# A selective scan on Trainium2: the residual added by TensorE and kept by ScalarE, and three of 16 states weighted by VectorE

## The reference

```python
x = x + _L0_attn_b_ref(_layernorm(x), ...)

# within it, for each batch row:
dt = softplus(dt_unproj @ W_dt.T + b_dt)
u = silu(conv(x @ W_x.T)); z = x @ W_z.T
A_tilde = exp(dt[..., None] * A)                    # 16 states for each of 256 channels
B_tilde = (A_tilde - 1.0) / (A + 1e-10)
h = A_t * h + B_t * Bp_t[:, None, :] * u_t[:, :, None]   # over time
y_t = einsum('bn,bdn->bd', Cp_t, h)                 # sum over the 16 states
y = (y + u * D_param) * silu(z)
return y @ W_out.T                                  # then added to x
```

## Time and profile before

| | us |
|---|---|
| three runs | 2103.42, 2104.65, 2106.32 (median 2104.65) |
| the profiled execution | 2105.05 |
| its span, first to last instruction | 2103.3 |
| the scan's loops, first ring input to last add | 1264.8 to 1849.7 |

### The profile page before, as it was taken

The page is one execution under the profiler, slowest core; times in us unless marked ns, Lnnn a source line. Parts: engine busy times, 40 slices in busy tenths (PEclk is TensorE's granted clock), DMA queues, the critical chain, the costliest instruction groups (busy, mean ns, idle before and its releaser), DMA issues. The chain is left out here.

```text
span 2103.3 us, 25351 instructions
## 1 busy us (share of the span) xinstructions
PE 1938.0 (92%) x6834; PEld 728.0 (35%) x6834; DVE 1676.9 (80%) x2442; ACT 1062.5 (51%) x1399; POOL 755.2 (36%) x517
## 2 busy tenths in 40 slices
PE   8997999999999999999999997788888988799997
PEld 4441332322232323322444443233333333244443
DVE  5889998998998988964565578999999999945554
ACT  3541666665666666672222236576557557422221
POOL 4662110000000000000100029999999999810000
PEclk9996999999999999999999998999999989999998
DMA  3652112321211121213100013444444445300000
GB/s 103 142 128 52 41 42 45 66 45 42 42 47 42 41 47 41 41 50 118 40 0 0 0 62 92 125 114 118 117 115 116 117 117 152 88 0 20 20 10 31
DMA packets 94539, 138.23 MB, mean 66 GB/s; under 512 B 13600, under 2 KB 52656, under 8 KB 92880
## 3 DMA queue, kind: packets, MB, share of 16 engines
q1 hardware_dynamic: 94416, 136.73, 26.1%
HBM read 110.21 MB, written 26.08 MB: 65 GB/s over the span
## 5 line engine op out<-in xcount | busy, mean ns | idle before, releaser
L915 DVE TENSOR_REDUCE mx<-max_bank 128x1 f32<-128x512 f32 x960 | 617.9, 686 | 64.6 <-PE max_bank L824 64.3
L901 ACT ACTIVATE probs<-score_bank 128x1024 f32<-128x1024 f32 x512 | 496.9, 1021 | 289.2 <-PE score_bank L838 289.0
L824 PE MATMUL max_bank<-ks,qs 96*128 96x512 bf16 x960 | 335.6, 390 | 0.0
L838 PE MATMUL score_bank<-qs,ks 99*128 99x512 bf16 x1024 | 313.2, 389 | 14.9 <-issue 10.2
L1700 POOL TENSOR_TENSOR ring<-u,bc 128x1024 f32<-128x1024 f32 x128 | 302.6, 2374 | 0.0
L1770 PE MATMUL ys_bank<-outs,rec_diag 128*128 128x512 f32 x512 | 253.9, 626 | 45.6 <-POOL outs L1708 23.0
L884 PE MATMUL o_bank<-probs,vg 128*32 128x512 f32 x2048 | 275.4, 610 | 0.7 <-ACT probs L901 0.7
L1708 POOL TENSOR_TENSOR outs<-ring,bc 128x1024 f32<-128x1024 f32 x109 | 258.7, 2373 | 26.3 <-DVE ring L2079 26.3
L784 POOL CAST neg_parts<-neg_max 16x128 bf16<-16x128 f32 x31 | 8.8, 282 | 656.9 <-DVE neg_max L928 656.9
L1935 ACT ACTIVATE a_bank<-dt,decay_s 128x512 f32<-128x512 f32 x256 | 169.4, 684 | 147.4 <-DVE ring L2079 105.6
L1451 ACT ACTIVATE relu_f<-hid_bank_f 128x512 f32<-128x512 f32 x128 | 76.5, 597 | 327.3 <-PE hid_bank_f L1376 282.3
(11 more groups left out here) (216 smaller groups left out, 2149.4 us busy)
## 6 DMA issues: line engine op xcount, KB each, us to landing
bc<-bc_scr SPq DMA_DIRECT2D x128, 512.0 KB, 4.9
qk_parts<-parts SPq DMA_DIRECT2D x128, 96.0 KB, 1.9
qs<-qk_parts SPq DMA_DIRECT2D x128, 64.0 KB, 4.1
o_scr<-o_sb SPq DMA_DIRECT2D x32, 256.0 KB, 2.1
ks<-qk_parts SPq DMA_DIRECT2D x16, 384.0 KB, 4.7
xin<-in_x_dram SPq DMA_DIRECT2D x8, 512.0 KB, 3.9
ks<-qk_parts SPq DMA_DIRECT2D x16, 256.0 KB, 3.5
qs<-qk_parts SPq DMA_DIRECT2D x32, 128.0 KB, 4.7
```

The costliest lines, as they stand in the source:

```text
L824: nc.tensor.matmul(max_bank[(r + a) % MB][:], qs[r][0:SROWS, half, j, qt * P:(qt + 1) * P], ks[r][0:SROWS, j, kh * TW:(kh + 1) * TW], star ...
L838: mm = nc.tensor.matmul(score_bank[pair][:, j % 2], ks[r][0:MROWS, j, kt * P:(kt + 1) * P], qs[r][0:MROWS, qh, j, :], start=True, stop=True)
L901: nc.scalar.activation(probs[:, s % 2, 2 * pair:2 * pair + 2], score_bank[pair][:], ACT.Exp, scale=SOFTMAX_SCALE).then_inc(probs_ready, 1)
L915: nc.vector.tensor_reduce(mx[:, a // HU, a % HU:a % HU + 1], max_bank[(r + a) % MB][:], AX_X, ALU.max)\
```

## The change

The output projection gets a third pair, the identity times x, so that the bank holds x + out. ScalarE copies it to x (`keep_x`) where VectorE added before; it stands in ScalarE's order in the same units. VectorE weights three units of tiles 0 to 6 in place of two, and others. The last tile's list stays.

```diff
-    ON_DVE, ON_DVE_LAST = (3, 5), (3, 6, 9, 12, 15)
+    ON_DVE, ON_DVE_LAST = (4, 7, 9), (3, 6, 9, 12, 15)
...
             def out(t, c, bank):
                 pe.wait_ge(gated, DC * t + DC)
-                product(bank[:], [(wout[:, f, c * P:(c + 1) * P], gy[:, f]) for f in range(DC)], out_made)
+                product(bank[:], [(ident[:], x_of(t, c))] + [(wout[:, f, c * P:(c + 1) * P], gy[:, f]) for f in range(DC)],
+                        out_made)
...
+            def keep_x(t, c, bank):
+                act.wait_ge(out_made, DC * t + c + 1)
+                nc.scalar.activation(x_of(t, c), bank[:], ACT.Copy).then_inc(x_new, 1)
...
                     if t and n == 1:
                         guess(t + 1)
+                    if t >= TPB and n == 3:
+                        keep_x(t - 2, 1, w1)
+                    if not more and n in (5, 6):
+                        keep_x(t - 1, n - 5, (w0, w1)[n - 5])
...
                     if n == 13:
                         silu_z(t, 0, w1[:])
                         exp_tables()
+                    if t and more and n == 15:
+                        keep_x(t - 1, 0, w0)
                     if norm_more and n == 15:
                         square(t + 2)
...
             keep_state(UNITS - 1)
+            keep_x(NT - 1, 0, w0)
+            keep_x(NT - 1, 1, w1)
...
-            def add(t, c, bank):
-                dve.wait_ge(out_made, DC * t + c + 1)
-                nc.vector.tensor_tensor(x_of(t, c), bank[:], x_of(t, c), ALU.add).then_inc(x_new, 1)
```

More of the change, by code:

```diff
@@ L1606, in scan @@
         wz, wout, wtap, wpar, wdt, b_dt = (w[n] for n in ("wz", "wout", "wtap", "wpar", "wdt", "b_dt"))
+        ident = w["ident"]
         a_col, is_small = w["decay"][:, 1], w["decay"][:, 2]
@@ L2109, in tiles @@
                             gate(t - 1)
-                        if t >= TPB and n == 3:
-                            add(t - 2, 1, w1)
                         if more and n == 11:
@@ L2117, in tiles @@
                             centre(t + 2)
[L2118 to L2123, removed]
             with dve.If(small != 0):
@@ L2131, in _ @@
             gate(NT - 1)
-            add(NT - 1, 0, w0)
-            add(NT - 1, 1, w1)
 def lay_out(v):
```

## The result

The changed kernel takes 2136.85 us (median of six runs, 2132.70 to 2140.56) against 2105.21 for the kernel before in the same rounds: a ratio of 1.0151, with a 95% interval of 1.0140 to 1.0162. That is 31.6 us slower; 28 were forecast. The changed kernel is called after from here on.

What follows compares the result with a forecast made beforehand. The prediction took a loop of VectorE and ScalarE to pace the scan, with GpSimd having slack. Its terms, -0.4 + 24.6 + 6.5 - 4.2 + 1.6 = +28.1 us on 2105.05, gave 2133 us, range 2118 to 2148.

Steps and rivals of the forecast that it cites:

- The bound: In the scan, a loop of VectorE and ScalarE sets the pace; GpSimd has slack of some 3 us per tile.
- The blocked copy: Unit 15, tiles 1 to 6: ScalarE's copy waits for TensorE's product, delaying the next tile's first decays: +24.6 us.
- The rival of a TensorE that stays slow for longer: Lower clock reaching through z product and next sum, ahead of the output product: 2147 to 2153 us, chance 0.09.
- The unit behind it: Next unit's first decay, behind ScalarE's silu of z and two table loads: VectorE stalls about 1.08 us six times, +6.5 us.
- Moved weightings: VectorE's stalls at units 8, 11 and 12 shrink with the new list of weighted units: -4.2 us.
- the forecast of -1 for unit 8: At unit 8, x kept earlier frees bank w1 sooner, but VectorE has less work ahead: about -1 us in all.
- The end of the scan: Behind the scan, two three-pair products add 1.72 us and the last add of 0.69 becomes a 0.60 copy: +1.6 us.
- The sum: All terms over the kernel: -0.4 + 24.6 + 6.5 - 4.2 + 1.6 = +28.1 us.
- -0.4: On VectorE, seven more weightings (7.9 us) against 14 fewer adds (8.3 us): -0.4 us.

Runs made afterwards that it cites:

- e2_weights_only: The kernel before with only the new list of units weighted by VectorE (4, 7, 9 for 3, 5), adds left on VectorE: 2115.12 us, ratio 1.0048.
- e7_later_two: The changed kernel with ScalarE's chunk 0 copy moved to the next tile's unit 0 and VectorE weighting two units (3, 5): 2098.02 us, ratio 0.9961.
- e9_later_one: The changed kernel with the chunk 0 copy in the next tile's unit 0 and VectorE weighting one unit (9) in tiles 0 to 6: 2099.94 us.
- e1_copy_later: The changed kernel with ScalarE's copy of chunk 0 moved from unit 15 to unit 0 of the next tile: 2104.39 us, ratio 0.9989.
- e6_product_earlier: The changed kernel with TensorE's output product of chunk 0 in unit 14 in place of 15, ScalarE's order unchanged: 2113.34 us, ratio 1.0045.
- e3_residual_only: The changed kernel with the old list of units weighted by VectorE (3 and 5), so third product and copy alone: 2128.73 us, ratio 1.0113.
- e10_busy_before_mean: The changed kernel with seven products of a zero matrix ahead of the mean in each tile, keeping TensorE busy: 2117.81 us, ratio 1.0068.
- e5_no_identity: The changed kernel without the third pair, leaving out the scan's residual add; ScalarE copies the two-pair product over x: 2124.35 us, ratio 1.0097.

## Why the prediction was right

*The bound.* That VectorE and ScalarE set the scan's pace and GpSimd had slack held: e2_weights_only took work from GpSimd and lost time, e7_later_two took work from VectorE and gained; and only when GpSimd had one more weighting per tile, in e9_later_one, did VectorE wait for it by more than 1.4 us.

*The blocked copy.* Shown from three sides: moved behind other work, the loss is gone (e1_copy_later); with the product earlier it shrinks to 4.4 us (e6_product_earlier); it is there without the new list (e3_residual_only). The forecast was 24.6 us at unit 0, 3.6 to 5.0 each, behind a wait of ScalarE of 6 to 8.6; measured were 27.8, 4.45 to 4.79 each, and 8.57 of waiting in tile 2. Tile 2, forecast with a slow mean and a slow sum, was 5.0 against 4.79; the other five were forecast with the faster sums of the kernel before (mean and sum 5.0 to 6.1 us) and came out as slow as tile 2 (6.4 to 6.6). So the mechanism was right and TensorE's clock mis-sized by 5.9 us over six tiles, in the one execution profiled. Two things went the other way: ScalarE's copy and squares back to back took 1.53 us rather than 1.72, 1.1 us in all, and VectorE wanted the decays 0.1 to 0.5 us later after the mean's start than in the kernel before, 1.5 us in all: 24.6 + 5.9 - 1.1 - 1.5 = 27.9. Without these two this term would have been off by 5.9, not 3.2. The rival of a TensorE that stays slow for longer did not take place: the slow stretch reached through the unit sum in all six tiles, but the granted clock is 1.00 again from the z product on. Of the Trainium skill's two statements ("TensorE: Matmul & The Clock Gate"), that activity releases the low clock (the part on the HAM clock gate) agrees with e10_busy_before_mean; its figure of about 216 ns for a matmul of 512 columns (Back-to-back issue gap) does not give the price of the float32 pair, which took 0.86 us as two records.

*The unit behind it.* 6.5 forecast, 5.9 measured.

*Moved weightings.* Forecast -4.2: units 11 and 12 gave -3.0 (1.6 and 1.2 us in even and odd tiles, to the digit), units 6 to 8 -0.7. The sum was near, but units 6 to 8 also hang on the clock of the taps, as tiles 2 and 4 of e2_weights_only show; I had not seen that. In after the granted clock from the first tap to the silu of u was 0.99 to 1.00 in tiles 1 to 6; before it was 0.87, 0.92 and 0.85 in tiles 3, 5 and 6. At full clock the wait at unit 8 is longer with the change, 1.52 us in even tiles from 2 on and 0.91 to 0.96 in odd ones against 0.99 and 0.61. So the forecast of -1 for unit 8, argued from the earlier x, came near by luck.

*The end of the scan.* Two third pairs in TensorE's order and the last copy, against the earlier trace rows:

```profile
1878.44 1.10 PE L1725 MATMUL work<-xT,ident_s 128*128 128x512 f32 x2 [1.48 <-DVE gy L2062]
1879.37 1.88 PE L1725 MATMUL work<-gy,wout_s 128*128 128x512 f32 x4
1881.09 1.02 PE L1725 MATMUL work<-xT,ident_s 128*128 128x512 f32 x2
1881.95 1.88 PE L1725 MATMUL work<-gy,wout_s 128*128 128x512 f32 x4
...
1883.86 0.60 ACT L1927 ACTIVATE xT<-work 128x512 f32<-128x512 f32 x1 [1.98 <-PE work L1725]
```

From the first product to the last one's end are 5.39 us in place of 3.67: +1.7, and the copy 0.60 in place of 0.69, as forecast.

*The sum.* -0.4 + 27.8 + 5.9 - 3.7 + 1.6 = 31.2; VectorE's waits for the mean ahead of `centre` grew from 1.5 to 2.6 us, which was not forecast: 32.3. The profiled executions, from which these are read, differ by more, 34.9 us: 33.4 in the scan (584.8 and 618.2 us from the first ring input to the last write of x) and 1.5 ahead of it. The 1.1 us of the scan still open are VectorE's scans and scales, which took 1.2 us more in all. Measured are 31.6 by medians. After's profiled execution is a slow one of its six, at a mean granted clock of 0.938 where the fastest two had 0.945, so the 5.9 us for the mean and sum are likely at the high end.

## What to carry to other kernels

An instruction moved to an idle engine can cost what it waits there, and not what it takes: look up when its input is there on the old engine, and what stands behind it in the new engine's order. The add was just in time on VectorE because VectorE came to it late; ScalarE came to the copy some 8 us before its product, and the decays that VectorE needed next were queued behind it. And an even load of two engines doesn't say which one binds: ask which of them waits for the other.

## What the runs showed of the hardware

TensorE's granted clock was 0.50 under the mean (3.6 us) and 0.57 under the sum (3.0 us) behind a wait of 6.48 us in after, and 1.00 in the same place when the wait was 0.91 us (e10_busy_before_mean). The length of mean and sum behind nearly equal waits varied between runs and tiles: 4.95, 5.51 and 6.47 us all behind waits of 6.5 to 6.6 us (tile 1 of e5_no_identity, tile 2 of e2_weights_only, tile 1 of after); and in e9_later_one it was 6.3 us in all six tiles behind waits of 5.2 to 5.3. So the length of the wait alone does not tell it. What decides between these was not found.

The record of GpSimd's weighting has no fixed length: 2353 ns in after, 2373 before, and 2408 in e9_later_one (groups of instructions: mean ns of one, idle before):

```profile
L1709 POOL TENSOR_TENSOR outs<-ring,bc 128x1024 f32<-128x1024 f32 x102 | 240.0, 2353 | 72.5 <-DVE ring L2089 72.2
```

```profile
L1709 POOL TENSOR_TENSOR outs<-ring,bc 128x1024 f32<-128x1024 f32 x116 | 279.4, 2408 | 5.2 <-DVE ring L2089 5.2
```

But GpSimd's pace does not change with it. Its next record starts before the last one ends, and from one start to the next, where it did not wait, are 2.31 us on average in all three. Nor is the record longer the less GpSimd waits: in e7_later_two it had 2355 ns and 17.3 us of waits, before 2373 and 26.3. What sets its length was not found. The scan of e9_later_one took 580.7 us from the first ring input to the last copy, where 573.6 had been the least; of the 7.1 us more, 5.2 are GpSimd's waits, and 1.3 that its last instruction ends 11.3 us before the scan does, not 10.
